# A graph layer and a mixture-of-experts layer on one core: PSUM banks cleared by VectorE instead of a zero product, and the last token lists made on the chip instead of through DRAM

## The reference

```
gnn(H):  HW = H @ W;  out[n] = sum over edges e with src[e] = n of edge_weight[e] * HW[dst[e]]
         relu(out + bias)                     16384 edges, 1024 nodes
ffn(x):  scores = sigmoid(x @ Wg.T + bg);  (w, idx) = top_k(scores, 2);  w = w / sum(w)
         nx = normalized x;  for each of 64 experts e, for its tokens:
           h = silu((nx*gamma_e + beta_e) @ W1_e + b1_e) * ((nx*gamma_e + beta_e) @ W3_e + b3_e)
           y += w_e * (h @ W2_e + b2_e)       512 -> 256 -> 512, f32
         shared expert: z = (silu(nxs @ Ws1 + bs1) * (nxs @ Ws3 + bs3)) @ Ws2 + bs2
x = x + gnn(layernorm(x));   x = x + ffn(layernorm(x))
```

## Time and profile before

| | |
|---|---|
| median of 3 runs | 474.7 us (474.32 to 475.35) |
| the profiled execution | 474.9 us, its span 473.1 us |
| busy in the span: PE, PEld, DVE, ACT, POOL | 403.6, 206.5, 200.8, 165.2, 139.9 us |
| TensorE's granted clock over the span | 0.928 |
| DMA | 126.10 MB, mean 267 GB/s |

### The profile page before, as it was taken

How to read it: one execution, slowest core, us unless ns; L and a number is a source line. 1 busy time by engine, 2 the same in 40 slices (tenths; PEclk the granted TensorE clock), 3 DMA queues, 4 the chain that set the end, 5 groups by cost and what they waited for, 6 DMA issues and landing times.

```text
span 473.1 us, 6490 instructions
## 1 busy us (share of the span) xinstructions
PE 403.6 (85%) x1829; PEld 206.5 (44%) x1830; DVE 200.8 (42%) x663; ACT 165.2 (35%) x406; POOL 139.9 (30%) x228
## 2 busy tenths in 40 slices
PE   2899999999999976599999999988889698897700
PEld 1676666665565543234444434433334333343200
DVE  5866567213757677433332333332131321313036
ACT  9868878332223120033333323332222222222100
POOL 2584344003243453403332233332131311301000
PEclk9989999999999995689999999999899988999765
DMA  4999400010101763259999999999999999997158
GB/s 109 340 402 409 196 0 0 2 40 24 44 23 27 286 184 129 54 193 402 407 403 406 410 405 405 407 407 409 406 408 408 404 407 405 408 399 312 43 201 333
DMA packets 41778, 126.10 MB, mean 267 GB/s; under 512 B 7953, under 2 KB 8529, under 8 KB 41618
## 3 DMA queue, kind: packets, MB, share of 16 engines
q1 hardware_dynamic: 35954, 117.29, 63.9%
q0 software_dynamic: 5792, 8.43, 5.0%
HBM read 121.22 MB, written 13.39 MB: 284 GB/s over the span
## 4 chain that ended last, share of the span: by engine, by line
PE 80%; DVE 5%; DMA 5%; issue 5%; SPq 2%; ACT 1%; ACTq 0%; POOL 0%; DVEq 0%; POOLq 0%
PE bank L1188 28%; PE bank L1205 12%; PE bank L1096 12%; PE bank L1059 7%; PE bank L1066 6%; PE bank L1197 5%; PE bank L1181 3%; PE bank L1056 2%; DMA X<-in_x_dram 2%; PE bank L1084 2%; PE bank L1115 1%; DMA w<-totals 1%; DVE X L1002 1%; DVE X L1001 1%; DMA A<-nx_rows,A 1%
## 5 line engine op out<-in xcount | busy, mean ns | idle before, releaser
L1188 PE MATMUL bank<-w,xhT 128*64 128x512 f32 x368 | 92.5, 649 | 15.1 <-issue 14.2
L956 DVE SCALAR_TENSOR_TENSOR osl<-bank,b13T,osl 128x64 f32<-128x64 f32 x132 | 28.5, 277 | 171.5 <-ACT osl L626 171.4
L619 ACT COPY xh<-bank 128x512 f32<-128x512 f32 x33 | 19.3, 585 | 155.1 <-PE bank L1188 155.1
L1096 PE MATMUL bank<-HW,AT 128*128 128x512 f32 x128 | 57.3, 593 | 0.0
L1188 PEld LDWEIGHTS bank<-w,xhT 128*64 128x64 f32 x368 | 28.7, 147 | 62.3 <-issue 59.8
L1205 PE MATMUL bank<-w,osl 128*64 128x512 f32 x184 | 45.4, 612 | 3.0 <-DVE osl L956 3.0
L501 POOL DMA_INDIRECT totals<-osl,A x17 | 17.3, 1017 | 96.0 <-PE bank L1181 76.4
L540 ACT ACTIVATE osl<-iota,eT 128x128 f32<-128x128 f32 x128 | 39.0, 388 | 12.1 <-PE bank L1059 12.1
L501 POOL DMA_INDIRECT totals<-GW,A x16 | 16.2, 1015 | 85.0 <-PE bank L1181 69.5
L497 POOL DMA_INDIRECT A<-nx_rows,A x33 | 33.8, 1025 | 16.1 <-issue 9.8
L1096 PEld LDWEIGHTS bank<-HW,AT 128*128 128x128 f32 x128 | 23.3, 190 | 23.9 <-issue 23.9
(11 more groups left out here) (197 smaller groups left out, 538.9 us busy)
## 6 DMA issues: line engine op xcount, KB each, us to landing
w<-in_L_ffn_W_dram SPq DMA_DIRECT2D x66, 1024.0 KB
A<-in_L_ffn_W_dram SPq DMA_DIRECT2D x15, 1024.0 KB
HW<-in_L_ffn_W_dram SPq DMA_DIRECT2D x10, 1024.0 KB
AT<-in_L_ffn_W_dram SPq DMA_DIRECT2D x5, 1024.0 KB
w<-totals SPq DMA_DIRECT2D x8, 512.0 KB, 7.3
w<-in_L_ffn_W_dram SPq DMA_DIRECT2D x6, 512.0 KB
X<-in_x_dram SPq DMA_DIRECT2D x4, 512.0 KB, 7.1
out_dram<-X SPq DMA_DIRECT2D x8, 256.0 KB, 5.6
```

What stands on the lines that cost most here:

```text
L956: ins = v.scalar_tensor_tensor(hT[b][:, m, CAP * h:CAP * h + CAP], bank[4][:, (HC + m) * P + CAP * h:(HC + m) * P + CAP * h + CAP], b13T[: ...
L1096: ins = t.matmul(bank[4 + s % 2][:, :], AT[:, s % 2, k, :], HW[:, k, :], start=(k == 0), stop=(k == NB - 1))
L1188: ins = t.matmul(bank[2 + b][CAP * h:CAP * h + CAP, :], xe[b][:, c, CAP * h:CAP * h + CAP], up_w[v][:, h, :, c, :], start=(c == 0), stop=( ...
```

## The change

- L1056 goes, and with it `zeros`. VectorE clears a bank's 384 columns with a memset ahead of each quad's sum (four at the start, then one in each `sums`); TensorE waits for the count `zeroed` instead of a_chain, and its four products all have `start=False`.
- The lists of blocks 0 to 5 still go through DRAM; their head is loaded while block 7 is routed. For blocks 6 and 7 VectorE makes a one-hot `place` of each token's place in its list, POOL a product `value` of the expert one-hot and the record less NOWHERE, and TensorE multiplies them (`list_slots`) into a bank, which VectorE adds to the turned list (`listed_first`, `listed_last`). Their records go to DRAM later, after the first four gathers.
- Routing: the scores' part comes first on VectorE (`vr_ready`), without the reciprocal: the two largest of -(1 + exp) are taken, and shares 0 and 1 change places. The shared expert's part follows (`vs_ready`, `es_ready`, `hs_ready`). POOL makes the stack (`stacked`, five instructions) that VectorE made with three, and one instruction fewer in the deviations.
- TensorE: `rank` comes after the sixth of eight products of `sum_messages` and no longer after the eighth, `transpose_nx` behind it; the stack's transpose (`transpose_stack`) has its own place, a block later. `transpose_a` uses two banks instead of four.
- SyncE: the lists' load stands ahead of the write of block 7's `nx`, and the sixth slot's load behind it.
- All eight `add_shared` stand behind `listed_last`. `turn_rows(0, 0)` no longer waits for them.

```diff
             def sums(r, j, q, start=False):
                 dve.wait_ge(quad_done[q % 2], done + (q // 2 + 1))
                 dve.wait_ge(a_chain, done * 2 + (q + 4))
+                if not start:
+                    v.memset(bank[(q - 1) % 4][:, 0:QW], 0.0).then_inc(zeroed, 1)
                 v.tensor_tensor(to, to, bank[q % 4][:, 0:QW], ALU.add).then_inc(a_chain, 1)
...
+                    if with_x and first and q == 0:
+                        for b in range(2):
+                            v.memset(bank[b][:, 0:QW], 0.0).then_inc(zeroed, 1)
+                    if with_x and first and q == 2:
+                        dve.wait_ge(raw_evac, 4)
+                        for b in range(2, 4):
+                            v.memset(bank[b][:, 0:QW], 0.0).then_inc(zeroed, 1)
...
-                        pe.wait_ge(a_chain, quad + (q + 1))
-                        t.matmul(bank[q % 4][:, 0:QW], ones[0:1, 0:P // 2].bitcast(bf16),
-                                 zeros[0:1, :].unsqueeze(1).broadcast_to([1, QW // 64, 64]), start=True, stop=False)
+                        pe.wait_ge(zeroed, quad + (q + 1))
...
# POOL
+            def values(t):
+                i = t % 2
+                pool.wait_ge(mk_ready, t + 1)
+                g.tensor_tensor(value[i], oh[i].unsqueeze(2).broadcast_to([P, 2, REC, 64]),
+                                shifted[:, t, :, :].unsqueeze(3).broadcast_to([P, 2, REC, 64]), ALU.mult).then_inc(value_ready, 1)
+            def stacked(t):
+                i = t % 2
+                if t >= 2:
+                    pool.wait_ge(stack_ps, t - 1)
+                pool.wait_ge(share_ready, t + 1)
+                pool.wait_ge(hs_ready, t + 1)
+                g.tensor_tensor(hsig, vr[:, 64:96], sg, ALU.mult)
+                g.tensor_scalar(weighted, oh[i][:, 0, :], share[:, t, 1:2], None, ALU.mult)
+                link(g.tensor_scalar(other, oh[i][:, 1, :], share[:, t, 0:1], None, ALU.mult))
+                g.tensor_tensor(stack[i][:, 64:96], hsig, vr[:, 96:128], ALU.mult)
+                g.tensor_tensor(stack[i][:, 0:64], weighted, other, ALU.add).then_inc(stack_ready, 1)
+            for s in range(NB + 1):
+                if s < NB:
+                    deviations(s)
+                if s > DRAM_BLOCKS:
+                    values(s - 1)
+                if s >= 1:
+                    stacked(s - 1)
+                if 1 <= s <= DRAM_BLOCKS:
+                    scatter_records(s - 1)
...
# VectorE, route
-                mark(v.tensor_tensor(vr[:, 64:128], route_bank[t][:, 64:128], bc[:, 64:128], ALU.add))
                 link(v.scalar_tensor_tensor(vr[:, 0:64], route_bank[t][:, 0:64], ratio[:, t:t + 1], bc[:, 0:64], ALU.mult, ALU.add))
-                v.tensor_scalar(er, vr[:, 0:96], -87.0, None, ALU.max).then_inc(vr_ready, 1)
+                v.tensor_scalar(er[:, 0:64], vr[:, 0:64], -87.0, None, ALU.max).then_inc(vr_ready, 1)
+                if t:
+                    dve.wait_ge(stack_ready, t)
+                link(v.tensor_tensor(vr[:, 64:128], route_bank[t][:, 64:128], bc[:, 64:128], ALU.add))
+                v.tensor_scalar(er[:, 64:96], vr[:, 64:96], -87.0, None, ALU.max).then_inc(vs_ready, 1)
                 dve.wait_ge(er_ready, t + 1)
-                link(v.tensor_scalar(er, er, 1.0, None, ALU.add))
-                link(v.reciprocal(sg, er))
+                link(v.tensor_scalar(gate, er[:, 0:64], 1.0, -2.0 ** -10, ALU.add, ALU.mult))
+                link(v.max(m8, gate))
...
+                v.tensor_scalar(share[:, t, :], m8[:, 0:2], rsum, None, ALU.mult).then_inc(share_ready, 1)
+                dve.wait_ge(es_ready, t + 1)
+                link(v.tensor_scalar(er[:, 64:96], er[:, 64:96], 1.0, None, ALU.add))
+                v.reciprocal(sg, er[:, 64:96]).then_inc(hs_ready, 1)
...
# VectorE, order
             for s in range(1, NB + 2):
                 if s <= NB:
                     relu_add(s - 1)
+                if 3 <= s <= NB:
+                    stack_out(s - 3)
                 if s >= 2:
                     route(s - 2)
                     if s == NB + 1:
-                        for b in range(3):
-                            add_shared(b)
+                        listed_first()
                     rank(s - 2)
+            listed_last()
+            stack_out(NB - 2)
+            dve.wait_ge(count_ps, 1)
...
-            for b in range(3, NB):
+            for b in range(NB):
+                if b == 4:
+                    stack_out(NB - 1)
                 add_shared(b)
...
# TensorE, order of a block and of the tail
                     sum_messages(s, range(0, 2))
+                    if s >= 3:
+                        transpose_stack(s - 3)
                     route(s - 2)
-                    sum_messages(s, range(2, 8))
+                    sum_messages(s, range(2, 6))
+                    rank(s - 2)
+                    transpose_nx(s - 1)
+                    sum_messages(s, range(6, 8))
...
+            route(NB - 2)
+            transpose_stack(NB - 3)
             pe.wait_ge(at_ready, 2 * NB)
-            route(NB - 2)
-            for b in range(3):
+            for b in range(4):
                 shared(b)
             transpose_nx(NB - 1)
             rank(NB - 2)
             route(NB - 1)
+            transpose_list()
+            list_slots(NB - 2)
+            shared(4)
             rank(NB - 1)
-            for b in range(3, NB):
-                shared(b)
-            pe.wait_ge(list_in, 16)
...
+            list_slots(NB - 1)
+            transpose_stack(NB - 2)
+            pe.wait_ge(list_ready, 1)
+            t.matmul(list_bank[0:64, 128:129], C, ones[:, 0:1], start=True, stop=True).then_inc(count_ps, 1)
+            shared(5)
+            shared(6)
+            transpose_stack(NB - 1)
+            shared(7)
```

More of the change, by code:

```diff
@@ L139, in moe_gnn @@
         before = GW[:, 0, 256:384]
+        place = [a.rearrange("p (k n) -> p k n", k=2) for a in (GW[:, 0, 384:512], eT[:, 2, :])]
+        value = [a.rearrange("p (k a e) -> p k a e", k=2, a=REC) for a in (
+            route_buf[:, 256:512], eT[:, 0:2, :].rearrange("p a t -> p (a t)"))]
+        listed = GW[:, 1, 448:512]
+        other = route_buf[:, 1856:1920]
+        shifted = stats[:, 0:NB * 2 * REC].rearrange("p (s k a) -> p s k a", k=2, a=REC)
         stackT = [GW[0:97, 2 + i // 4, 128 * (i % 4):128 * (i % 4) + 128] for i in range(NB)]
@@ L240, in moe_gnn @@
         route_ps, vr_ready, er_ready = sem("route_ps"), sem("vr_ready"), sem("er_ready")
-        stack_ready, rank_ps, stackT_ready = (sem(s) for s in (
-            "stack_ready", "rank_ps", "stackT_ready"))
+        vs_ready, es_ready, hs_ready = sem("vs_ready"), sem("es_ready"), sem("hs_ready")
+        mk_ready, share_ready, value_ready = sem("mk_ready"), sem("share_ready"), sem("value_ready")
+        stack_ready, stack_ps, stackT_ready = sem("stack_ready"), sem("stack_ps"), sem("stackT_ready")
+        rank_ps, place_ready, c_ready, list_ps, listed_ready = (sem(s) for s in (
+            "rank_ps", "place_ready", "c_ready", "list_ps", "listed_ready"))
         z_ps, z_added = sem("z_ps"), sem("z_added")
@@ L324, in _ @@
                 if s == NB - 2:
+                    for i in range(2):
+                        sp.wait_ge(rec_out[i], 32 * DRAM_BLOCKS // 2)
+                    sp.wait_ge(x1_ready, NB)
+                    sp.dma_start(L, lists[:, :, 0:CAP * REC]).then_inc(list_in, 16)
+                if s == NB - 1:
                     sp.wait_ge(out_ps, NB)
@@ L353, in _ @@
                     sp.wait_ge(tokens_ready, 1)
+                    for i in range(2):
+                        sp.wait_ge(rec_out[i], 32 * NB // 2)
                     load_over(0)
@@ L477, in _ @@
                                  fill=0.0, base=0, channel_multiplier=-1))
-            for s in range(NB + 2):
-                if s < NB:
[L482 to L491, removed]
+            pool.wait_ge(consts, 8)
@@ L506, in _ @@
                 gather(TOK[:, j:j + 1], j)
+            pool.wait_ge(list_in, 16)
+            for s in range(DRAM_BLOCKS, NB):
+                scatter_records(s)
             for j in range(PAIRS + 1):
@@ L782, in sum_pair @@
                     if q >= BEHIND:
-                        sums(r, j, q - BEHIND)
+                        sums(r, j, q - BEHIND, with_x and first and q == BEHIND)
                     elif not first:
@@ L1214, in down_of @@
                 down(j, j % 2, j % SLOTS)
+            pe.wait_ge(xg_in[0], 16)
+            turn_rows(0, 0)
+            pe.wait_ge(extra_ready, 1)
             pe.wait_ge(z_added, NB)
```

156 lines of the change are left out of this document (90 added, 66 removed).

## The result

| | before | changed |
|---|---|---|
| median | 474.5 us (474.1 to 475.4, 4 runs) | 458.2 us (455.7 to 460.3, 4 runs) |
| ratio to before, 95% interval | | 0.963 (0.959 to 0.968) |
| the profiled execution, its span | 474.9, 473.1 us | 458.8, 457.1 us |

16.3 us faster, where 13.4 was forecast. Its rivals stand in each expectation.

The account below looks back on a forecast made before the run. TensorE's instructions were taken to bound the adjacency and message stages, the weight stream the loop's end. Gains of 6.6 (adjacency) and 6.8 (tail) sum to 13.4 us: median 474.7 to 461.3, forecast 459.5 to 463.5 (0.52), range 457.5 to 467.

Parts of the forecast that it names:

- Loop, one for one: Expert loop: moving the start of `up(0)` moves the first refill, the weight stream and the end by the same amount.
- the zero product's price: Adjacency stage: the zero product holds 0.26 us per quad, so 28 quads give 7.3 us.
- Its cover: Adjacency stage: VectorE's 0.40 us memsets fit its idle time, 0.7 us left per half pair; 0.3 us booked for unevenness.
- Start-up: First quads: memsets ahead of the first M tiles and of quad 2 lose 0.4 us.
- Message stage, nothing: Message stage: TensorE's work per block stays the same, no gain booked; the wait for `Mk` covered by 0.9 us.
- Tail: From T, the last message product's end, to `up(0)`: T + 23.6 instead of T + 31.3; gain 6.8 us.
- (c): Tail: VectorE's route(7) newly waits for POOL's stack of block 6, values taking 1.1 us; VectorE loses 0.7 us.
- (f): Tail: all eight `add_shared` now follow listed_last; with shared products at the lower clock, the last addition ends at T + 22.1.
- VectorE as the pace of the adjacency stage: Rival: a memset costs 0.55 us or more and waits are uneven; stage gives 3 us, 465 us; chance 0.13.
- rival 3: Tail: TensorE keeps its full clock and values is cheap; 459 us; chance 0.12.
- POOL held up by VectorE: Rival: POOL's moved work takes twice as long; 3 to 4 us lost in the tail, 465 us; chance 0.14.
- POOL as the pace of the message stage: Rival: POOL's round passes the 9.5 us block, reaching 11.7 to lose all gain; 476 us and above; chance 0.06.

Follow-up runs that it names:

- e11: Changed kernel plus 10 unused TensorE products ahead of each weight wait in the last 15 pairs, 26 before the last down; 455.2 us, ratio 0.957.
- e12: Changed kernel plus early first memsets, new tail order, 16 unused products in the tail and the loop fillers of e11; 454.6 us, ratio 0.957.
- e10: Changed kernel plus 26 unused bf16 products of 256 columns on TensorE in the tail's gaps; 456.2 us, ratio 0.959.
- e9: Changed kernel with POOL's five stack instructions made twice for every block; 461.7 us.

## Why the forecast was right in kind and short by 3 us

- **Loop, one for one.** Right, by the distances just told. In e11 and e12 the chain itself names the weights (`DMA w<-in_L_ffn_W_dram`) as what the last `up` waited for; before it was only "issue".
- **Adjacency stage, the zero product's price.** The step that failed: "so much of each quad the zero product holds", 0.26 us. It measured 0.45. I took the distance from the zero product's start to the passes' start and left out what it does to the passes behind it and ahead of it: 0.1 between the first two passes and 0.1 between the last pass and the next zero product. The right reading was at hand in the rows of before: quads stood 1.35 apart, and eight passes of the same shape in `transpose_a` and `route` take 0.87 to 0.89 in the chain; the difference is 0.46 to 0.48. (In most blocks the passes of `transpose_a` take 0.92, which still gives 0.43.)
- **Its cover.** Memset 0.378 us, booked 0.40. But "0.3 more for unevenness" was far too small: 28 quads x 0.45 are 12.6 us, and 9.6 came (seven half pairs in 55.74 us, 7.96 each, against 9.34). The prediction had the term at hand: ScalarE is idle 1.5 us per half pair, "of which 0.5 is left". That holds for a half pair that gets 1.0 shorter; with 4 x 0.45 = 1.8 it is overdrawn, and 9.34 - 1.5 = 7.84 is near the 7.96 measured. The two errors had opposite signs, 5.3 and 2.7 us; that the sum was only 2.6 off is luck. VectorE's cover was also read too large (of the 26.9 us idle ahead of L761 the row puts 23.6 down to TensorE), without effect.
- **Start-up**, 0.4 lost: it lost 0.41, in part by luck, as profiles with the same start-up reach this point up to 1.1 us apart. TensorE's wait grew by 1.5 in this profile and by 0.6 to 1.0 in the five others, as it also had less to do before it.
- **Message stage, nothing.** Right: blocks are 9.67 apart (112.99 to 122.66), as before. `rank` found its `Mk`.
- **Tail.** Booked T + 23.6, measured T + 23.39, with single terms off and cancelling. The new wait (c) did not happen: `values` took 0.61 us, not 1.1, and the stack was ready at 167.86, 0.8 before VectorE came to it (168.62). The estimate from the Trainium skill (GPSIMD Engine Reference, "Elementwise — side-by-side cycle accounting") was 0.6 to 0.7; the trace agrees. list_ready came at T + 12.5 (booked 13.75), the gather at T + 13.45 (14.6). Nothing of that reached `up(0)`, because (f), the additions and the products at the lower clock, ended last, as forecast: the last addition at T + 21.6 (booked 22.1).
- **The rivals.** VectorE as the pace of the adjacency stage: no; at the waits looked at above its tiles and its memset were done 2 us ahead of the quad, and ScalarE was last. The measured 458.2 lies beside rival 3's 459, but not by its way: `values` was cheap, the full clock in the tail was not there. POOL held up by VectorE: L454's price of 0.445 held for the moved instructions (0.47 and 0.45 on average for 64 columns), so the exclusive port of the Trainium skill (SBUF — State Buffer, "Who interferes with whom") cost nothing that these rows show. The full clock in the tail did not come by itself; e10 made it for most of the tail, and `up(0)` came 2.7 us earlier. POOL as the pace of the message stage: e9 shows it was more than 1.7 us per block away.

## What to carry to other kernels

Price an instruction that is to be removed by the distance between its neighbours with and without it, from end to start on both sides, and look for the same neighbours elsewhere in the trace without it; start to start on one side misses what it does to the instructions on the other. Then set the saving against the idle time of every engine that feeds the stage, the untouched ones too: here ScalarE's 1.5 us per half pair capped a saving of 1.8. Before work is moved to another engine to get rid of an instruction, try to make the instruction itself cheap: 128 rows in place of one brought the same as VectorE's memsets. And where a stream of transfers sets the end, look first at two places, the start of the stream and what stands behind its last transfer, the latter at the full clock if the engine is kept at work while it waits.

## What the runs showed of the hardware that was not expected

- A bf16 product with one row of weights (1 x 128) among f32 products of 128 rows held 0.45 us; the same with 128 rows 0.16 to 0.17, as much as a second one-row product directly behind the first. Not shown: whether the type has a part in it.
- MEMSET of 384 f32 columns into PSUM by VectorE: 378 ns in all 31 cases, near the line through 112 ns for 64 and 59 ns for 1 in SBUF.
- On GpSimd a tensor_tensor of 256 columns took 0.61 us, of 64 columns 0.32, but a tensor_scalar of 64 columns 0.44 to 0.49 (all in the tail of the changed kernel).
- Filler products on TensorE held the granted clock at 1.00 from 171 to 177 us, where it fell to 0.81 and 0.50 without them, and `up(0)` came 2.7 us earlier; in the loop they held it at 1.00, and what stands behind the last weights took 3 us less.
